# Spreading the side work of a one-core attention kernel over other units of its blocks

## The reference

```python
x = x + 0.5 * ffn(layernorm(x))      # first feed-forward
x = x + attn(layernorm(x))           # k, q layernormed per head, causal softmax, Wo, bo
x = x + 0.5 * ffn(layernorm(x))      # second feed-forward

# ffn(x): base_W x + base_b, a shared pair of rank 16, and six routed pairs of rank 16;
#         softmax gate, top 2 of 6, weights normalised to one
# attn: dot = q k^T * scale, causal mask, softmax, times v
```

## Time and profile before

| what | us |
|---|---|
| median of three runs | 1348.42 (1347.44 to 1353.62) |
| the profiled execution, whole time | 1348.32 |
| its span, first to last instruction | 1346.6 |
| PE busy | 1165.6 (87%) |
| ACT busy | 1021.1 (76%) |
| DVE busy | 454.8 (34%) |
| POOL busy | 235.0 (17%) |
| granted share of the TensorE clock, mean | 0.954 |

### The profile page before, as it was taken

One profiled execution on the slowest core, in us unless ns is written; L12 is line 12 of the kernel. 1 busy time (PEld: TensorE's weight loads), 2 busy tenths in 40 slices (PEclk: granted clock), 3 DMA queues, 4 the chain that ended last, 5 costly groups with the idle time before them and its releaser, 6 DMA issues.

```text
span 1346.6 us, 23146 instructions
## 1 busy us (share of the span) xinstructions
PE 1165.6 (87%) x9076; PEld 385.2 (29%) x9076; DVE 454.8 (34%) x1164; ACT 1021.1 (76%) x1132; POOL 235.0 (17%) x377
## 2 busy tenths in 40 slices
PE   2636778999899979999899999899999999999974
PEld 2522323333232323322223223222222222222223
DVE  4655534445244424343233232322222111011113
ACT  2213546778688868888888899798999999999960
POOL 2223422323112210121101102101102101010000
PEclk9767988999899989999999999999999999999986
DMA  4011200101200030000300002100001200000000
GB/s 130 1 53 35 72 1 24 57 1 36 77 1 1 25 88 1 1 1 25 87 1 2 1 0 72 40 1 1 1 1 39 58 0 2 8 9 1 9 9 16
DMA packets 39674, 33.39 MB, mean 25 GB/s; under 512 B 8787, under 2 KB 39497, under 8 KB 39561
## 3 DMA queue, kind: packets, MB, share of 16 engines
q1 hardware_dynamic: 37360, 31.74, 7.9%
q10 hardware_dynamic: 2200, 0.12, 0.1%
HBM read 18.73 MB, written 12.85 MB: 23 GB/s over the span
## 4 chain that ended last, share of the span: by engine, by line
PE 62%; ACT 14%; DVE 10%; issue 7%; SPq 2%; DMA 2%; POOL 1%; ACTq 1%; DVEq 0%; POOLq 0%
PE ps L1101 56%; ACT ring L708 14%; PE ps L1140 2%; PE ps L1201 1%; DVE xnT L780 1%; SPq L540 1%; PE ps L1309 1%; DMA x<-in_x 1%; DVE oT L1081 1%; DVE st L739 1%; DVE xnT L778 1%; PE ps L1317 1%; PE ps L1160 1%; DVE area L760 1%; DVE area L934 1%
## 5 line engine op out<-in xcount | busy, mean ns | idle before, releaser
L708 ACT ACTIVATE ring<-ps 128x1024 f32<-128x1024 f32 x1056 | 989.7, 1103 | 166.5 <-PE ps L1101 163.9
L1101 PE MATMUL ps<-ring,vf 128*17 128x512 f32 (+3 forms) x4608 | 564.8, 568 | 3.8 <-POOL ring L662 2.9
L1101 PE MATMUL ps<-queries,keys 50*128 50x512 f16 (+3 forms) x2304 | 379.2, 369 | 35.6 <-DMA queries<-shift_d 9.8
L1101 PEld LDWEIGHTS ps<-queries,keys 50*128 50x128 f16 x2304 | 93.5, 93 | 505.1 <-ACT ring L708 433.4
L662 POOL TENSOR_SCALAR_AFFINE_SELECT ring<-ring 128x256 f32<-128x256 f32 (+1 forms) x224 | 98.4, 457 | 462.9 <-ACT ring L708 461.5
L1101 PEld LDWEIGHTS ps<-ring,vf 128*17 128x17 f32 x4608 | 80.3, 96 | 174.5 <-issue 145.7
L778 DVE CAST xnT<-ps 128x512 f16<-128x512 f32 x50 | 34.5, 690 | 126.0 <-PE ps L1140 110.8
L649 POOL TENSOR_TENSOR rstd<-var,minus_half 128x4 f32<-128x4 f32 x24 | 24.4, 1016 | 268.6 <-DVE var L745 268.5
L1081 DVE COPY oT<-ps 128x512 f32<-128x512 f32 x32 | 22.1, 690 | 144.9 <-PE ps L1101 144.9
L1101 PE MATMUL ps<-baseT,xnT 128*128 128x256 f16 x384 | 56.7, 287 | 7.6 <-DVE area L780 1.8
L912 DVE SCALAR_TENSOR_TENSOR x<-ps,power,x 128x512 f32<-128x512 f32 x32 | 24.0, 750 | 113.9 <-PE ps L1101 113.9
(11 more groups left out here) (145 smaller groups left out, 704.0 us busy)
## 6 DMA issues: line engine op xcount, KB each, us to landing
parts_d<-split SPq DMA_DIRECT2D x32, 256.0 KB, 2.6
keys<-parts_d SPq DMA_DIRECT2D x96, 64.0 KB, 2.3
queries<-parts_d SPq DMA_DIRECT2D x192, 32.0 KB
x<-in_x SPq DMA_DIRECT2D x8, 512.0 KB, 4.0
out_x<-x SPq DMA_DIRECT2D x16, 256.0 KB, 2.2
queries<-shift_d SPq DMA_DIRECT2D x64, 4.0 KB
ring<-in_base_W SPq DMA_DIRECT2D x1, 256.0 KB, 3.9
ring<-in_Wq SPq DMA_DIRECT2D x1, 256.0 KB, 4.9
```

The costliest lines, as they stand in the source:

```text
L708: act.activation(probs[:, u % RING, :], bank(2 * (u % SLOTS), 2), ACTF.Exp, bias=0.0, scale=1.0).then_inc(exp_ok, 1)
L1101: return pe.matmul(o, lhsT, rhs, start=start, stop=stop, skip_group_check=True)
```

## The change

Two numbers of `schedule` change. From block 3 on, `front` and `prepare` of the next block begin six units later (and still end at u1 - 12). In blocks 2 to 6, `back` ends at u1 - 20 instead of u1 - 2. All steps are the same, and so are all instructions; their order on the engines is another.

```diff
@@ -181,14 +181,14 @@
             ahead = front(0, 0, c + 1) if c >= LONG else ()
-            lists.append(spread(itertools.chain(ahead, prepare(c + 1)), u0, max(u1 - 12, u0 + 6)))
+            lists.append(spread(itertools.chain(ahead, prepare(c + 1)), u0 + 6 if c >= LONG else u0, max(u1 - 12, u0 + 6)))
...
         behind = [c - 2] if 2 <= c < NC - 1 else [c - 2, c - 1] if c == NC - 1 else []
         if behind:
-            lists.append(spread(itertools.chain(*map(back, behind)), u0 + 10, u1 - 2))
+            lists.append(spread(itertools.chain(*map(back, behind)), u0 + 10, u1 - 2 if c == NC - 1 else u1 - 20))
```

## The result

The changed kernel takes 1331.43 us, median of four runs (1329.93 to 1332.86), where the kernel before, in runs beside it, took 1350.03. The ratio is 0.986, with a 95% interval of 0.9832 to 0.9888: 1.4% faster. The forecast was 1331, from a profiled execution of 1348.3. The profiled execution of the changed kernel took 1331.12 us, with a span of 1329.4 against 1346.6: 17.2 us less.

What follows compares the result with a forecast made beforehand. PE and ACT were taken to pace the attention part together, with waits for x at the starts of blocks 3 to 6. Sum: 1348.3 - 20.9 + 2.7 + 1.0 = 1331.1 us, range 1326 to 1337 (74%).

Steps and rivals of the forecast that it cites:

- What bounds the kernel, and the chain: Attention part: PE and ACT pace together; at starts of blocks 3 to 6 late x delays moments0, division, turnout, then exponentials.
- 20.9 us at the starts: Starts of blocks 3 to 6: waiting removed, 15.9 us PE standstill, 1.2 behind masks, about 3.8 slower clock and refilling.
- the second rival: Starts of blocks 3 to 6: only PE's 15.9 us standstill comes back, clock falls elsewhere; 1336 us, chance 10%.
- Either edit alone: Starts of blocks 3 to 6: either edit takes most of the wait; the first leaves 2 to 3 us in block 4.
- the fourth rival: Block starts: moments0 still waits for x because SP is late, 2 to 3 us in two blocks; 1336 us, chance 4%.
- New pairs, 2.7 us: Blocks 2 to 6: closer PE side steps on one PSUM bank add three waits of 0.9 us; bounds 0 to 5.5.
- cover for slack, 1.0: Blocks 2 to 6: back packed earlier hides less of PE's spare time; 1.0 us added, bounds 0 and 4.
- The third rival: Block 4 near 620 us: the clock also stops falling there, new pairs cost nothing; 1325 us, chance 5%.
- work behind the last exponential is unchanged: Sign for the changed trace: work after 1300.8 us is unchanged.
- moments0 beside projout at nothing: Block's seventh unit: moments0's 1.41 us on DVE beside projout costs nothing; without cover at most 5.6 us in four blocks.
- The DMA engines: Load of x beside writes of 256 KB: 4.0 us to land, 8 us at worst by the shared-engine rule, still in time.
- The slower rival: Middles of blocks 2 to 6: crowding drops the clock, 3.3 us per same-unit pair; 1348, up to 1363; chances 5%, 1%, 1%.

Runs made afterwards that it cites:

- e3_load_only: The kernel before with only the load moved, to three units behind the last outer1 in blocks 2 to 6; 1341.97 us, ratio 0.9932.
- e2_back_only: The kernel before with the second edit only: back ends at u1 - 20, front begins at the block's first unit as before; 1329.45 us, ratio 0.9838.
- e5_front_apart: The kernel before with the first edit only, plus PE's side steps in blocks 2 to 6 kept two units apart; 1320.81 us, ratio 0.9785.
- e4_apart: The changed kernel with PE's side steps in blocks 2 to 6 kept two units from each other and from a division; 1316.95 us, ratio 0.9743.
- e10_back_apart: e4_apart without the first edit: front and prepare begin at the block's first unit, back ends at u1 - 20; 1318.40 us, ratio 0.9769.

## Why the prediction was right, and where

**What bounds the kernel, and the chain.** The steps held one by one: late load, moments0 waiting, the division behind it, turnout on PE behind that, then empty score slots. e3_load_only moves nothing but the load; it takes 8.1 us of waiting away and 9.1 us off the starts.

**20.9 us at the starts.** The comparison with blocks 2 and 7 gave 22.0, less 1.1 for turn0; the starts gave back 22.1, and turn0 is in the middle of block 3 now (+2.8 us there, with the new pairs). The like-for-like number is that of e2_back_only, 20.6. Two pieces inside were off and cancel: turn0 is 1.6 us of the start and not 1.1 (17.40 against 15.80; the row of four transposes that gave the 1.1 is another step's, read while the clock was low), and the wait is 14.7 us of idle PE and 5.9 of slower matmuls, where the prediction split it into 17.1 and 3.8. Counting PE's idle time alone (15.9 us, the second rival) would have fallen short. The experiments price the difference. For a short wait of DVE the start grows by somewhat less than the wait, for 1.42 and 1.60 us by 0.8 and 0.9; for the long ones by more, for 5.86 us by 6.6 and for 7.57 by 8.7. The clock makes the difference: it was 0.85 and 0.79 over these two starts. Blocks 5 and 6 of the kernel before say the same of two waits of like size: 3.24 us at a clock of 1.00 cost 2.7, and 2.94 us at 0.91 cost 3.3 (18.65 and 19.34 against e2_back_only's 15.92 and 16.06).

**Either edit alone.** Right, but the rest of 2 to 3 us in block 4 that I gave to the first edit was not there. I had put moments0 six to eight us after the start; it is read 9.2 us after it (496.67 for 487.47), because the six units at a block's start are slow ones, with turnout and projout. What this hid is that the margin is near zero, as e5_front_apart showed. The other margin was put too high as well: the load was to go out ten units or more, over 9 us, before the next block, and went out 8.3, 5.4, 8.0 and 11.7 us before blocks 3 to 6, since SP was behind the order, the case that the fourth rival had named. In block 4 x landed only 1.0 us before the block began. This cost nothing, because moments0 comes later still.

**New pairs, 2.7 us, and cover for slack, 1.0.** The middles cost 2.3 us in all; less the 1.1 of turn0 that is 1.2 (0.7 with the measured 1.6), where 3.7 had been forecast. The price of a pair is confirmed by e4_apart; what was missed is that block 4's middle got 2.6 us shorter. There the crowded place near 620 us no longer slows the clock (1.00 over the whole middle). The third rival had this in part; but a fall near 892 us, in block 6, came in its place. The 1.0 us for slack is not priced by itself; the 0.7 us between the middles of e4_apart and e5_front_apart, which have no pairs, are the nearest to it.

**The sum.** It came out to the microsecond by luck: the middles were 2.5 us too dear in the forecast, and 2.6 us appeared in stretches that the change does not touch. The prediction's sign that the work behind the last exponential is unchanged held for the work and not for its time, 1.6 us more at a clock of 0.60 against 0.66. Executions of one order differ by as much: blocks 0 and 1, in the same order, took 154.8 to 154.9 us in seven profiles and 156.2 or 156.3 in four.

**moments0 beside projout at nothing.** Held: the starts have the 15.8 to 16.1 us of blocks 2 and 7. e10_back_apart against e4_apart says the same.

**The DMA engines.** From issue to landing, the four earlier loads took 4.2 to 4.7 us, against 3.8 to 3.9 among fetches alone; and SP's wait for a write of split halves rose at the longest from 3.4 to 4.5 us:

```profile
SPq L528 <- DMA parts_d<-split: 43.1, 16, 4.5
```

This is what the Trainium skill says in "DMA: Bandwidth & Descriptors", section "Issuing engines are not separate DMA queues", that DMAs share the engines and interleave; the trace agrees, at 0.4 to 1.1 us a piece and not at double. No engine that computes waits for it.

**The slower rival.** A cost of 3.3 us for each of six pairs was far too high. Removing 6 pairs in one unit and 15 a unit apart gave 14.5 us in all.

## What to carry to other kernels

Where all engines follow one written order, look at the first instruction that reads a loaded buffer and ask what stands behind it on its engine: here statistics of the next block that nobody needed yet held up a division that everything needed. To price such a stall, compare the elapsed time of the stretch with a stretch of the same work without it, not the idle time of one engine: here 20.6 us, and 22 with the step that moved out, against 15.9. And give the load its margin on the queue that issues it, since every gain elsewhere eats a margin that is only just enough (e5_front_apart); then look at the neighbours on a shared bank, which here were worth nearly as much as the change (e4_apart, 1317 us; with the later division 1316 us, which is the same within their spread).

## What the runs showed of the hardware

The granted clock behind the last exponential was 0.60 in two profiles of one order and 0.70 in two of another, with the same instructions in that stretch, and this alone made 2.6 us. A standstill of PE of 5.1 us was followed by a start at a clock of 0.85 (e5_front_apart), while starts with the 0.2 to 0.6 us waits of the changed kernel stayed at 1.00. Between them the length of the standstill does not decide it: in the kernel before, 2.79 us at the start of block 5 left the clock at 1.00, and 2.49 us at the start of block 6 were followed by a fall to 0.91 over the start. PE's timeline there:

```profile
668.65 0.63 PE L1317 MATMUL ps<-ident,att 128*128 128x128 f32 x4 [2.79 <-DVE att L1088]
...
857.58 0.63 PE L1317 MATMUL ps<-ident,att 128*128 128x128 f32 x4 [2.49 <-DVE att L1088]
```

In the kernel before, SP took 0.28 to 0.46 us to issue each DMA around the end of block 3, one behind the other, and the load that the order places three units before the block's end left 6.1 us after it.
